# First attention loop of a two-block fusion network: convolution as banded products, scores over 32 rows, output spread over the copies, zero rows under the inverse

## What is computed

```
qkv = xp @ w_qkv;  q, k, v = split(qkv);  q = q * SCALE
q_l = mean of q over groups of positions;  k_l = the same of k
attn1 = softmax(q @ k_l.T);  attn2 = softmax(q_l @ k_l.T);  attn3 = softmax(q_l @ k.T)
z = attn2.T / (col * row)                      # col, row: largest sums over the whole batch
for _ in range(6):
    az = attn2 @ z
    z = 0.25 * z @ (13*I - az @ (15*I - az @ (7*I - az)))
out = attn1 @ z @ (attn3 @ v) + conv33(v, res_kernel)     # a filter of 33 taps per head, along positions
out = x + out @ w_out + b_out
```

## Time and profile before

| | |
|---|---|
| median of 3 runs | 934.46 us (930.55 to 937.0) |
| profiled execution | 928.29 us, its span 926.5 us |
| TensorE, VectorE, ScalarE, GpSimd busy | 805.0, 526.2, 360.4, 278.2 us |
| first stage | 0 to about 77 us; VectorE's last instruction at 76.3, the shift of XC issued at 72.4 and 4.6 us to land |
| tap building in it | TensorE 9.6 us (L510), GpSimd 7.5 us (WOK) |
| setup | 77 to 154.3 us |
| loop over batches | 154.3 to 510.4 us |
| the rest (expert layer, second attention, second expert layer) | 510.4 to 926.5 us |

### The profile page before, as it was taken

How to read it: one execution, slowest core, us unless ns; L and a number is a source line. 1 busy time by engine, 2 the same in 40 slices (tenths; PEclk the granted TensorE clock), 3 DMA queues, 4 the chain that set the end, 5 groups by cost and what they waited for, 6 DMA issues and landing times. The chain is left out here.

```text
span 926.5 us, 18263 instructions
## 1 busy us (share of the span) xinstructions
PE 805.0 (87%) x5604; PEld 583.6 (63%) x5604; DVE 526.2 (57%) x1039; ACT 360.4 (39%) x820; POOL 278.2 (30%) x280
## 2 busy tenths in 40 slices
PE   3475778999899999999999759996899999996797
PEld 0134558687778786878787646673666666645565
DVE  3463782658484837585754543334476766755343
ACT  1032232334333424343422346663455555532343
POOL 8701222243343323433344311222222222203111
PEclk9996775899999989999999769997699999995699
DMA  6001000000000000000000000000000000000000
GB/s 225 0 1 27 1 2 0 1 2 1 2 0 0 0 1 1 0 0 1 1 2 1 1 1 0 0 0 0 1 2 1 0 0 0 1 1 1 0 12 13
DMA packets 4478, 7.03 MB, mean 8 GB/s; under 512 B 3528, under 2 KB 3528, under 8 KB 4104
## 3 DMA queue, kind: packets, MB, share of 16 engines
q1 hardware_dynamic: 3992, 2.38, 1.1%
q10 hardware_dynamic: 432, 4.00, 1.1%
HBM read 5.21 MB, written 0.55 MB: 6 GB/s over the span
## 5 line engine op out<-in xcount | busy, mean ns | idle before, releaser
L951 POOL TENSOR_TENSOR TD<-SA,NN 91x492 f32<-91x492 f32 (+1 forms) x96 | 105.4, 1113 | 189.3 <-issue 76.5
L747 PEld LDWEIGHTS PS<-ST 91*91 91x91 f32 x768 | 84.7, 162 | 19.4 <-issue 11.8
L747 PE MATMUL PS<-ST 91*91 91x123 f32 x768 | 94.9, 276 | 1.1 <-ACT ST L878 1.1
L747 PE MATMUL PS<-NN 91*91 91x123 f32 (+1 forms) x768 | 92.4, 274 | 4.0 <-DVE NN L1053 4.0
L1053 DVE SCALAR_TENSOR_TENSOR NN<-ST,PS 91x492 f32<-91x492 f32 x96 | 63.4, 662 | 55.0 <-PE PS L747 46.9
L747 PEld LDWEIGHTS PS<-NN 91*91 91x91 f32 x768 | 84.1, 165 | 15.4 <-DVE NN L1053 7.6
L886 ACT ACTIVATE SA<-ST 91x492 f32<-91x492 f32 (+1 forms) x96 | 51.5, 565 | 99.1 <-DVE ST L1061 99.1
L1621 DVE TENSOR_SCALAR CL<-PS,K 128x270 f32<-128x270 f32 x144 | 65.8, 495 | 17.9 <-ACT EX L1567 7.0
L1061 DVE SCALAR_TENSOR_TENSOR ST<-PS,TD 91x492 f32<-91x492 f32 (+1 forms) x96 | 57.3, 602 | 32.6 <-PE PS L747 29.5
L1515 PE MATMUL PS<-QR,KA 128*128 128x270 f32 x256 | 73.7, 412 | 0.0
L1567 ACT ACTIVATE EX<-CL,NG 128x540 f32<-128x540 f32 x64 | 47.3, 740 | 40.8 <-DVE CL L1621 40.8
(11 more groups left out here) (297 smaller groups left out, 1549.8 us busy)
## 6 DMA issues: line engine op xcount, KB each, us to landing
MB<-mat ACTq DMA_DIRECT2D x1, 2304.0 KB, 12.6
WI<-wide ACTq DMA_DIRECT2D x1, 1051.0 KB, 5.9
XC<-XC SPq DMA_DIRECT2D x1, 607.8 KB, 4.6
MA<-mat ACTq DMA_DIRECT2D x1, 550.0 KB, 7.2
out<-OS SPq DMA_DIRECT2D x8, 45.0 KB
CO<-const SPq DMA_DIRECT2D x1, 324.0 KB, 3.7
XA<-xpatch SPq DMA_DIRECT2D x1, 256.0 KB, 2.8
CO<-const SPq DMA_DIRECT2D x1, 256.0 KB, 3.0
```

The source lines that it names most:

```text
L747: last = nc.tensor.matmul(PS[0:NL, 4 + 2 * n + q, (h % 4) * SW + c0:(h % 4 + 1) * SW], x[:, h, 0:NL], x[:, h, c0:SW], start=True, stop=True)
L951: nc.gpsimd.tensor_tensor(TD[:, 4 * q:4 * q + 4, c0:SW], SA[:, 4 * q:4 * q + 4, c0:SW], NN[:, 4 * q:4 * q + 4, c0:SW], ALU.subtract).then_ ...
```

## The change

The loop is rebuilt:
- **Convolution.** The host builds a banded matrix of the filter for each head (`taps`, tile TP, 1.2 MB, loaded in the first stage), with the three copies folded onto the 71 + 71 distinct positions. `attend` multiplies the values VU with it, into the same bank as the attention's output. TAP, WOK, XW, the shift of XC and `taps` go.
- **Scores.** `scores3` and `scores1` contract 32 rows for each head, the four heads of a half in four row groups and four banks, as the landmark scores do; KM has no zeros and is copied by VectorE in one piece. One reduction (`top3`) takes the largest of all eight heads, two (`top1`) the others.
- **Output.** `attend` writes all 269 positions (the image part three times), OC takes them, and two output products follow, one in each half of the array's columns.
- **Order.** Attend, output products and residual of a batch are done in the next batch's steps 3, 5, 8 and 9 (`BACK`), and after the last one behind the loop. Banks 4 and 5 serve both kinds of steps. The loop over batches is written out, 8 bodies in a row, and the copies XS, XW and AS go.
- **Rows.** ST, NN, PT, UU, AA, P3 and VU have 128 rows, with zeros from the used ones on, and the products contract 128 rows.
- **Setup.** Four of the eight landmark heads are exponentiated straight from PSUM with their sums (`halved`); VectorE subtracts and sums only the other four. `weigh(0)` stands behind the last `sums`.

```diff
+                def scores3(b):
+                    pe.wait_ge(sem("f_q"), upto(b, 1, 1))
+                    pe.wait_ge(sem("f_k"), upto(b, 1, 1))
+                    pe.wait_ge(sem("f_vu"), upto(b, 1, 1))
...
+                    for hh in range(2):
+                        for r in range(4):
+                            rows = slice(32 * r, 32 * r + 32)
+                            last = nc.tensor.matmul(PS[0:NL, bank(b, r), hh * U:(hh + 1) * U], QM[rows, hh, U:U + NL],
+                                                    KM[rows, hh, 0:U], start=True, stop=True)
+                    last.then_inc(sem("f_s3"), 1)
+
+                def scores1(b):
+                    pe.wait_ge(sem("f_e3"), upto(b, 1, 1))
...
+                def turn3(b):
+                    pe.wait_ge(sem("f_sub1"), upto(b, 2, 2))
...
+                def attend(b, hh):
...
+                    for c, h in heads:
+                        nc.tensor.matmul(PS[c:c + 32, TAIL + hh, 0:COPIES * NI], UU[:, b % 2, h, :],
+                                         PT[:, b % 2, h, 0:NI].unsqueeze(1).broadcast_to([128, COPIES, NI]),
+                                         start=True, stop=False, skip_group_check=True)
...
+                    for c, h in heads:
+                        nc.tensor.matmul(PS[c:c + 32, TAIL + hh, 0:T0W], VU[:, b % 3, 0, h * DH:(h + 1) * DH],
+                                         TP[:, h, 0:T0W], start=False, stop=False, skip_group_check=True)
...
+                FRONT = {0: project, 1: values, 2: scores3, 4: scores1, 7: turn3, 9: weigh, 11: turn1}
+                BACK = {3: lambda b: attend(b, 0), 5: lambda b: attend(b, 1), 8: out_proj}
+
+                def body(b):
+                    for k in range(STEPS):
+                        step(b, k // 2, k % 2)
+                        if b and k in BACK:
+                            BACK[k](b - 1)
+                        if b + 1 < B and k in FRONT:
+                            FRONT[k](b + 1)
+                    if b + 1 < B:
+                        start(b + 1)
...
+                def exps3(b):
+                    act.wait_ge(sem("f_m3"), upto(b, 1, 1))
...
+                FRONT = {0: (key,), 1: (value,), 2: (top3,), 4: (total3,), 5: (top1, inverse3), 6: (shift1,), 7: (total1,),
+                         8: (inverse1,), 10: (small,)}
```

More of the change, by code:

```diff
@@ new lines, in scores1 @@
+                def scores1(b):
+                    pe.wait_ge(sem("f_e3"), upto(b, 1, 1))
+                    for hh in range(2):
+                        for t in range(2):
+                            for r in range(4):
+                                rows = slice(32 * r, 32 * r + 32)
+                                c = (2 * hh + t) * NL
+                                last = nc.tensor.matmul(PS[0:UT, bank(b, r), c:c + NL], QM[rows, hh, t * UT:(t + 1) * UT],
+                                                        KM[rows, hh, U:U + NL], start=True, stop=True)
+                    last.then_inc(sem("f_s1"), 1)
@@ L828, in _ @@
                 pe.wait_ge(sem("n_sub"), B)
+                pe.wait_ge(sem("n_half"), B)
                 nc.tensor.matmul(PS[0:NL, TOPS, 0:DH], ON[:, :], CG[:, :], start=True, stop=True).then_inc(sem("n_tops"), 1)
-                start(0, 0)
-                front(0, 0, 10)
-                front(0, 0, 11)
-                batches(pe, body)
+                start(0)
+                pe.wait_ge(sem("n_rck"), 1)
+                turn1(0)
+                for b in range(B):
+                    body(b)
@@ L919, in _ @@
+                    halved(i)
+                    if i == 7:
+                        act.wait_ge(sem("n_pad"), PADS)
+                    if i in ALONG:
+                        ALONG[i](0)
+                    if i + 1 < B // 2:
+                        copied(i + 1, 1)
+                turned1(0)
                 act.wait_ge(sem("n_rck"), 1)
-                batches(act, body)
+                for b in range(B):
+                    body(b)
+                attended(B - 1)
             @block.gpsimd
@@ L1117, in _ @@
                     summed(i)
[L1118 to L1120 removed]
+                    for work in ALONG.get(i, ()):
+                        work(0)
+                inverse3(0)
+                total1(0)
+                inverse1(0)
                 sums = PS[KP:128, SUMS, 0:B * H // DH * NL].rearrange("p (g n) -> p g n", n=NL)
@@ L1137, in _ @@
                 v.tensor_scalar(RCK[:, :], RC[:, :], SIG, None, ALU.mult).then_inc(sem("n_rck"), 1)
-                batches(dve, body)
+                for b in range(B):
+                    body(b)
+                residual(B - 1)
         phase_over()
```

762 lines of the change are left out of this document (350 added, 412 removed).

## The result

The changed kernel took 851.66 us in the median of four runs (845.83 to 862.59), the kernel before 935.54 beside it: 0.909 of its time, 95% interval 0.900 to 0.919. The forecast was 868, with a range of 848 to 898. The profiled execution was the slowest of the four, 862.59 for a span of 860.8. The forecast for that span was 860.7, which is less good than it looks: the setup was forecast 2.5 us too short and the loop 6.7 too long, the rest took 4.3 more than before, and the three cancelled.

The account below looks back on a forecast made before the run. TensorE's instruction stream was taken to bound the loop: 34.3 us of work plus 3.5 of waits a batch. Setup 10.8 and loop 55 less took the span from 926.5 to 860.7; the forecast was 868, range 848 to 898.

Parts of the forecast that it names:

- I take the zero rows at nothing: Inverse's products contracting 128 rows in place of 91: no added time, between -1 and +1 us a batch.
- TensorE's 34.3 us a batch: Attention loop: 29.1 us of TensorE work left, plus new scores 0.8 and 1.0, attend with convolution 2.8, output 0.6.
- together 14.4: TensorE work removed from a batch: taps 7.0, scores 2.9 and 2.2, old attend 0.7, output products 1.0 and 0.6 us.
- Waits of 3.5: TensorE's waits in a batch no longer hidden, at steps 4, 5, 6, 7 and the batch's end: 3.5 us in total.
- The loop, 301: Attention loop: first batch 42, six at 38 (228), last 25 plus 6; 301 us, 55 less than before.
- a stop like that at 253.76 costs a batch 3.8 us: VectorE's 3.48 us late start where the old loop returns, priced at 3.8 us for that batch.
- the rival at 935: Written-out loop, each instruction fetched once: two stops in every batch make it slower than before, 935 or more; chance 0.03.
- The setup, 10.8 less: Setup before the loop: first scores 5 us earlier, rounds 47, tail 13.4; loop begins at 143.5 in place of 154.3.
- No waits (853): Rival: filling covers all waits in the loop, a batch takes 34.5 to 36 us, kernel 853; chance 0.13.
- 6.2 under the median: Offset: the profiled run of the kernel before lay 6.2 us under its median, so 862.5 became the forecast 868.
- Waits take over (896): Rival: VectorE's in-order blocks and slow small operations beside GpSimd make a batch 42 us, kernel 896; chance 0.18.
- Tiles don't overlap (888): Rival: row-group score products run serially, or tile changes cost more than 0.16 us; +20 us, kernel 888; chance 0.06.

Follow-up runs that it names:

- before_zero_rows: Kernel before, loop written out, and its inverse's products contracting 128 rows, zeros included, in place of 91; 0.9874 of the kernel before, loop 340.8 us.
- tail_in_own_batch: Changed kernel with attend, output products and residual back at the end of their own batch; 862.6 us profiled, loop 309.3, batch 40.10.
- no_zero_rows: Changed kernel with products contracting only the rows that hold data (91, 71) in place of 128; 1045.6 us profiled, loop 487.2, batch 65.51.
- before_written_out: Kernel before with only its attention loop written out as eight bodies in a row; 1.0027 of the kernel before, loop 358.7 us.
- scores_in_turn: Changed kernel with both scores' products issued by row group, two or four in a row for the same 32 rows; 850.7 us profiled, batch 37.60.

## Why the prediction was right, and where it was not

**The size and its sources.** The loop's gain of 61.5 us (353.5 to 292.0) can now be taken apart by runs: 12.7 for what the clock and the loop's stops cost before (to `before_zero_rows`, 340.8), 17.3 for the order of the work (`tail_in_own_batch`, 309.3), and 31.5, the difference between these two, for TensorE's products and all else that was rebuilt in the loop. Of the 12.7, 5.0 lie in the first batch (49.1 before, 44.1 with zero rows, 0.86 and 0.96 of the clock). These shares hold to a few us, since the first batch's clock varies from run to run. The forecast had named all but the clock's part, and put the excess of the two batches behind the loop's returns, 6.1 us, down to these alone.

**"I take the zero rows at nothing"**: the step that failed most, though the sum did not show it. For the duration of the products it is right (1.77 us for eight with 128 rows and with 91). But a rival said "The zero rows do nothing. That is in the forecast.", and without them the kernel is slower than before, 1045.6 us. The forecast took the loop's granted clock of 0.97 over to a loop from which it had removed the taps and the wide scores, all products of 128 rows, and asked only what the new products cost. The Trainium skill (TensorE: Matmul & The Clock Gate, "What's actually happening") says that the gate goes by how busy TensorE has been; in `no_zero_rows` it was busy for 65.52 of 65.52 us and held at 0.50, so here the measurement decides: with the same products in the same order, the rows that they contract made the difference. The forecast came out right because the change itself brings what keeps the clock up, with which it had not reckoned; on this point it was luck.

**TensorE's 34.3 us a batch.** Measured: 35.48. The new forms were priced well, most a little high (scores 0.67 and 0.79 for 0.78 and 1.0; attend 2.2 for 2.8; output 0.67 for 0.6), 4.4 in place of 5.2 together. What failed was the subtraction, "together 14.4". Busy times of groups overlap: in the list of groups after, all of TensorE's groups together make 39.4 us, in a window with 35.48 busy. From start to start in batch 388.77 to 432.78 the work taken out was 13.0 (taps 6.3, scores 2.8 and 2.1, attend 0.7, output 1.1), which leaves 30.5. With the 4.4 that is 34.9, and the last 0.6 is in the work that stayed: the inverse's twelve steps take 0.9 more than before, the turns and the values 0.3 less. Part of the 0.9 is the going in and out of tiles: eight products take 1.86 from start to start ahead of attend and of scores1, and 1.70 to 1.82 ahead of other work. The forecast's own price for it, 0.16, was not a clean one, since the products of L667, which use no tiles, lie 0.10 over their columns too (1.05 for 0.95).

**Waits of 3.5.** Measured: 1.39 (36.87 less 35.48). The places were right: 0.9 at step 7 became 0.77, 0.9 at turn3 0.30, 0.5 at step 8 0.16, 0.8 at the batch's end 0.16, and 0.3 at the second scores none. The two errors, 1.2 too little of work and 2.1 too much of waiting, cancel in part: 37.8 forecast, 36.87 measured. What the step did not see is that the convolution lies beside a chain of ScalarE, GpSimd and VectorE and is free.

**The loop, 301.** Measured 294.3: 6.7 from batches of 36.87 in place of 38, 2.7 less in the first one (1.2 GHz for 5 us of it, not 14), and 2.7 more at the end, where the last attend ran at 1.2 GHz.

**The loop's return.** "VectorE came 3.48 us late ... just where the loop returns" was a true reading, and writing out removes the stops; that "a stop like that at 253.76 costs a batch 3.8 us" was not, as `before_written_out` shows: a stop costs 2.2 to 2.3, and the other 1.6 in that batch is the clock. No stop of the straight-line code appeared, which disposes of the rival at 935.

**The setup, 10.8 less.** The loop began 8.3 us earlier. The start, 5 earlier, was right (5.5). From the first scores to step 0 the forecast had 60.5 and the trace 63.8. The tail of 13.4 (measured 13.0) was right, and the four exponentials nearly (1.48 forecast, 1.25 from start to start); the 47 us for the rounds (50.8) left out that TensorE would work at the slow pace in most of them: six of the eight groups of scores took 0.97, one 0.86 and one 0.59.

**The rivals.** No waits (853) had 0.13, and the median is nearer to it than to 868. This is no support for its mechanism, since the waits are there. It comes from the offset, "6.2 under the median": the profiled execution of before was fast for its kernel, that of after slow for its own. Waits take over (896): no. Tiles don't overlap (888): no, and `scores_in_turn` shows what it would have cost.

## What to carry to other kernels

When a change removes work from TensorE, ask first what keeps its clock up, and look at the shapes of what is left: here 37 rows of zeros under the inverse's products are worth 196 us (1045.6 without, 849.8 with these alone). A busy share of 96% does not make an engine the bound where its work is filling; leave a piece out, and see whether the time moves. And never price a removal by adding up the busy times of groups: take starts.

## What the runs showed of the hardware that I had not expected

- In the same loop, with the same products in the same order, a batch ran at a granted clock of 0.50 where they contract 91 and 71 rows, and of 1.00 where they contract 128.
- In the kernel before, with 91 rows in the inverse, the clock fell in five of six middle batches once the loop's stops were gone, for 1.6 or 3.2 us each; with 128 rows in one of six.
- A VectorE operation on 8 elements with two inputs in SBUF, beside a GpSimd operation, lasts until that ends: 2.54 us for 0.16.
- Row groups overlap if neighbours in the queue differ: sixteen products in 0.79 us, in groups of four for the same rows 1.90; in pairs, eight in 0.68 for 0.67.
- The same setup code (but for the rows of weigh and of start in three runs) took 59.8 to 68.3 us. In the five runs with 59.8 to 62.8 the landmark scores first reached the fast pace in the second group, in the four with 68.2 or 68.3 in the fifth or sixth. In three of those four the granted clock read 1.00 for the slow stretch.
